# A one-core gated cross-attention and mixture-of-experts layer: reciprocals taken at step 19 of a turn instead of 13, and the sync queue's transfers in another order

## The reference, cut to what matters

```python
x = x + tanh(g_xattn) * xattn(layernorm(x), ctx)     # 32 batches of 128 x 512
x = x + tanh(g_ffn) * ffn(layernorm(x))

def xattn(x1, x2):                 # 8 heads of 16 channels, 512 positions, 128 channels
    q, k, v = proj(x1), proj(x2), proj(x2)
    attn = softmax(q @ k.T / 4)    # per head, 512 x 512
    return attn @ v

def ffn(x):                        # rmsnorm, router, top 2 of 8 experts, and a shared expert
    h = rmsnorm(x)
    return sum_of_top2(w_e * expert_e(h)) + shared(h)
```

## Time and profile before

| what | us |
|---|---|
| median of 3 runs | 1573.99 |
| lowest and highest of the 3 | 1565.47, 1575.32 |
| the profiled execution, its own time | 1563.96 |
| its span in the profile | 1562.1 |
| mean granted TensorE clock, as a share of the full one | 0.955 |

### The profile page before, as it was taken

The page is one execution under the profiler, slowest core; times in us unless marked ns, Lnnn a source line. Parts: engine busy times, 40 slices in busy tenths (PEclk is TensorE's granted clock), DMA queues, the critical chain, the costliest instruction groups (busy, mean ns, idle before and its releaser), DMA issues.

```text
span 1562.1 us, 25157 instructions
## 1 busy us (share of the span) xinstructions
PE 1411.3 (90%) x7290; PEld 669.2 (43%) x7290; DVE 1001.2 (64%) x2173; ACT 881.2 (56%) x1720; POOL 868.8 (56%) x1278
## 2 busy tenths in 40 slices
PE   4888899898998888888899989889999999999997
PEld 1122222222222222222222222226778888888886
DVE  5877677877787777777788777784675433333332
ACT  2467666775676666666677667673433433333333
POOL 7336655666566666566757664544321455555553
PEclk9999989998999999999999999999999999999999
DMA  5547555565766657567566666526655488976665
GB/s 168 155 137 197 160 170 161 170 178 154 155 168 172 168 157 157 150 174 183 163 164 180 169 153 149 143 98 196 143 138 174 93 215 206 221 177 129 110 112 83
DMA packets 161314, 247.94 MB, mean 159 GB/s; under 512 B 33606, under 2 KB 58829, under 8 KB 161183
## 3 DMA queue, kind: packets, MB, share of 16 engines
q1 hardware_dynamic: 138830, 208.43, 49.3%
q0 software_dynamic: 18256, 37.38, 12.8%
q10 hardware_dynamic: 4096, 0.53, 0.3%
HBM read 141.85 MB, written 103.88 MB: 157 GB/s over the span
## 4 chain that ended last, share of the span: by engine, by line
PE 43%; DMA 21%; issue 12%; POOL 7%; SPq 7%; DVE 5%; ACT 3%; POOLq 1%; ACTq 1%; DVEq 0%
PE bank L1409 15%; PE bank L1366 9%; DMA pv_d<-arena 7%; PE bank L1337 6%; SPq L466 6%; PE bank L1315 6%; DMA parts_k<-arena 4%; DMA arena<-m_rows 4%; DVE row_max L883 3%; DMA arena<-pv_d 3%; PE bank L1353 2%; POOL xs L768 2%; POOL arena L667 2%; POOL arena L664 2%; PE bank L1297 2%
## 5 line engine op out<-in xcount | busy, mean ns | idle before, releaser
L883 DVE TENSOR_REDUCE row_max<-bank 128x1 f32<-128x512 f32 x1024 | 670.9, 684 | 142.0 <-PE bank L1315 125.2
L1154 ACT ACTIVATE arena<-bank 128x512 f32<-128x512 f32 x1024 | 576.7, 603 | 321.6 <-PE bank L1337 310.6
L1337 PE MATMUL bank<-arena 112*128 112x512 bf16 x1024 | 331.5, 405 | 14.8 <-DMA arena<-m_rows 9.0
L1315 PE MATMUL bank<-arena 48*128 48x512 bf16 x1024 | 213.0, 412 | 105.0 <-DVE row_max L883 101.5
L1366 PE MATMUL bank<-arena 128*32 128x512 f32 x2048 | 297.3, 655 | 1.0 <-ACT arena L1154 0.7
L664 POOL TENSOR_TENSOR arena<-arena 128x512 bf16<-128x512 f32 x62 | 71.8, 1157 | 257.3 <-ACT arena L1146 254.8
L780 POOL DMA_INDIRECT out<-xs,ids x71 | 112.5, 1585 | 173.0 <-ACT xs L1238 138.1
L1337 PEld LDWEIGHTS bank<-arena 112*128 112x128 bf16 x1024 | 86.4, 103 | 252.5 <-ACT arena L1154 182.4
L1315 PEld LDWEIGHTS bank<-arena 48*128 48x128 bf16 x1024 | 49.6, 93 | 336.6 <-DVE row_max L883 258.0
L1409 PE MATMUL bank<-w_ring,h_hi 128*128 x568 | 183.0, 403 | 0.0
L1227 ACT ACTIVATE arena<-bank 128x256 f32<-128x256 f32 x103 | 39.5, 384 | 189.5 <-PE bank L1409 189.5
(11 more groups left out here) (176 smaller groups left out, 1981.3 us busy)
## 6 DMA issues: line engine op xcount, KB each, us to landing
pv_d<-arena SPq DMA_DIRECT2D x32, 512.0 KB, 4.7
w_ring<-split_d SPq DMA_DIRECT2D x60, 256.0 KB, 4.1
parts_k<-arena SPq DMA_DIRECT2D x96, 128.0 KB
arena<-parts_k SPq DMA_DIRECT2D x64, 192.0 KB
parts_q<-arena SPq DMA_DIRECT2D x96, 128.0 KB
arena<-parts_q SPq DMA_DIRECT2D x64, 192.0 KB
arena<-in_w SPq DMA_DIRECT2D x36, 256.0 KB, 4.6
arena<-in_ctx SPq DMA_DIRECT2D x32, 256.0 KB, 3.1
```

Of the source, the lines that this page charges most:

```text
L883: nc.vector.reduce_max(row_max[b % 2][:, at:at + 1], m_ps[(STEPS * b + u) % M_BANKS][:], AX_X).then_inc(s_mx, 1)
L1154: nc.scalar.activation(probs[group % 3][:, j, :], e_ps[n % E_BANKS][:], ACT.Exp, scale=float(DH) ** -0.5).then_inc(s_exp, 1)
L1315: nc.tensor.matmul(m_ps[(n + a) % M_BANKS][:], q_stack[b % 3][rows, h, qt * P:(qt + 1) * P], k_stack[b % 3][rows, h, :], start=True, stop= ...
L1337: nc.tensor.matmul(e_ps[n % E_BANKS][:], k_stack[b % 3][0:SHIFTED, h, kt * P:(kt + 1) * P], q_stack[b % 3][0:SHIFTED, h, :], start=True, s ...
```

## The change

`RECIP_AT` goes from 13 to 19, so VectorE's `invert` stands behind the maximum of step 19. There the loop first issues the reciprocal and then begins the rows of maxima for the same step. In each turn SP's order becomes: the queries' high part written, the values' product stored, the keys read, the queries' middle and low parts written, the denominators read, the queries read, context loaded, turned tokens stored, and only then the reciprocals stored and the values loaded. The amount of work and of data is the same.

```diff
-RECIP_AT = 13
+RECIP_AT = 19
...
             for i in TURNS:
                 if is_b(i + 2):
-                    read(i + 2, 0)
+                    write(i + 2, 1, HI)
                 if is_b(i - 1):
                     store_values(i - 1)
                 if is_b(i + 2):
-                    write(i + 2, 1, HI)
+                    read(i + 2, 0)
+                    write(i + 2, 1, MID)
+                    write(i + 2, 1, LO)
                 if is_b(i - 1):
                     load_denominators(i - 1)
                 if is_b(i + 2):
-                    write(i + 2, 1, MID)
-                if is_b(i - 1):
-                    store_reciprocals(i - 1)
-                if is_b(i + 2):
-                    write(i + 2, 1, LO)
+                    read(i + 2, 1)
                 if is_b(i + 4) and i + 4 >= 2:
                     load_ctx(i + 4)
                 if is_b(i - 3):
                     store_turned(i - 3)
-                if is_b(i + 2):
-                    read(i + 2, 1)
                 if is_b(i - 1):
+                    store_reciprocals(i - 1)
                     load_values(i - 1)
```

## The result

The changed kernel takes 1473.61 us (median of 4 runs, 1469.73 to 1477.03), against 1571.24 us for the kernel before on the same chip (4 runs, 1565.47 to 1575.32). The ratio is 0.938, with a 95% interval from 0.9337 to 0.9423: 6.2% faster. The forecast was 1465, inside a range of 1436 to 1515. The profiled execution took 1475.64 us, with a span of 1473.8, so its 88 us against the profiled execution of before can be followed in the trace.

The account below looks back on a forecast made before the run. PE, busy 90%, was held back by VectorE's reciprocal waiting for the denominators' DMA and by the low clock behind the pauses. 1563.96 - 104.7 (29 turns) + 3.1 (start) = 1462.4 us, put at 1465; range 1436 to 1515.

Parts of the forecast that it names:

- The reciprocal's wait: VectorE's wait for the denominators' DMA, 73.7 us in 25 waits, goes entirely at step 19, 3.9 us behind the landing.
- SP's order alone: With the new queue order but the reciprocal still at step 13, half a microsecond of its wait would be left.
- The pauses and the clock: PE's pauses behind the reciprocal's wait lower its clock; the mean over turns 1 to 29 rises from 0.93 to 0.98 or more.
- the sum from the other side: Cross-check of the gain: 73.7 us of reciprocal waits plus 65 us lost at the low clock, together 139 us.
- The turn: Turns 1 to 29 fall from 31.9 to 28.3 us each: 27.5 without pause plus 0.8 for new waits; 104.7 us less.
- turn 21: Check of 27.5: taken as a turn whose reciprocal did not wait; it took 29.40 us, 1.9 put down to pause and clock.
- the reciprocals' store: SP stores the reciprocals at 653.4 in turn 18, landing 1.4 us later; the values' load issues at 654.9 instead of 656.83.
- The start: Six key reads stand ahead of the queries' middle and low parts, delaying the first scores by 3.1 us; bounds 0 to 4.4.
- Turn 30 and the rest: Turns 30 and 31 and the experts' part keep their length, without key reads left or not using the changed lines.
- Rivals 1 and 2: Rows of maxima land late: at a turn's end (1485 to 1541 us, chance 0.17) or in mid-turn (1634 us, 0.05).
- rival 2: The first pair of rows of maxima lands behind the values' store, stopping PE for exponentials: 1634 us, chance 0.05.
- Rival 3: No change: the wait moves to step 19, or another loop as long as 31.9 us stands behind; 1563 to 1577, chance 0.04.

## Why the prediction was right, and where it was off

- **The reciprocal's wait.** The forecast had it near 0 at step 19. It went from 73.7 to 0.9 us. The working behind it was too optimistic: the denominators' read was forecast at T+9.4 and its landing at T+11.4. It was issued at T+10.9 in turn 17, and by the semaphore's events in the trace it landed 2.9 to 4.5 us behind its issue in turns 1 to 29, where it was 2.0 to 2.1 before. The margin at step 19 is 1.7 us in the median, and nothing at its least, instead of 3.9. The wait went because six steps left room for an error of some 2 us. The sentence that SP's order alone would leave half a microsecond fell: it left about 3.2 us in each turn, and 0.994 of the time.
- **The pauses and the clock.** Mean PEclk was forecast at 0.98 or more and came to 1.00. The low clock gave back 59.1 us of PE's busy time, where the sum from the other side had 65. The Trainium skill's "HAM oscillation" in "TensorE: Matmul & The Clock Gate" charges half of the throttled time; these traces agree with the charge within 10%. With all of the waits on top that working made 1428 us, and 1475.64 was measured, because waits came back in another place.
- **The turn.** Forecast 28.3 us, measured 28.57: 29 x 0.27 = 8 us short, the largest miss in the turns. The 0.8 us a turn that the forecast kept for new waits should have been 1.2 us over the 27.38 us at which the best turns of several kernels stand (it took 27.5 for that). That 27.5 was a good guess with a weak check: turn 21 is not one of the four whose reciprocal did not wait, for it waited 0.21 us. The four are turns 12, 16, 23 and 27, and they lasted 29.5 to 29.8 us. The step that failed is the reciprocals' store. It was forecast at T+16.3, landing after 1.4 us, and the load at T+17.8, sooner than before. It was in fact issued at T+18.5 and landed 4.2 us later, and the load went out at T+22.7, later than the T+19.7 of before (medians of turns 1 to 29: T+21.3 before, T+23.3 after). Two things were mis-sized. The query reads ended at T+17.4 (559.20) and not at T+15.4, since the key reads began 0.8 us later than forecast and took 4.92 us instead of 4.36, and the low part's write then took 2.8 us from its end to the first read (552.63 to 555.43) instead of 2.2. And 1.4 us was the landing of that small store with one write of a query part ahead of it in the queue, issued 1.7 us earlier; behind six reads SP's next issue, which waits for it, came 3.2 to 5.9 us later in turns 1 to 29. The forecast even claimed that POOL would get its load sooner. The run with the store in the middle bears on this term by changing it: beside the changed kernel on one chip it is worth 47 us. Of the 5.0 us by which the values' load was late against the forecast, 2.3 are the store's later issue and the rest its longer landing.
- **The start.** Forecast +3.1, measured +2.4 to turn 1. The first scores began at 32.47 us instead of 29.60, 2.9 us later, for the reason given: the six key reads stand between the query parts (the chain of waits and the timeline of PE). The forecast's 3.1 rests on a misread row: 19.09 is the start of the low part's issue, and the working set the end of the new one, 22.1, against it. Start against start it makes 21.5 - 19.09 = 2.4 us, and the new issue began at 21.65. That 3.1 came close to the 2.9 is luck.
- **Turn 30 and the rest.** The forecast kept them unchanged. Turn 30 grew by 4.8 us, and that was missed: the last load of values lands late there too, VectorE's moments wait 3.6 us for POOL, and PE, idle behind them, then runs at the low clock. The rows are VectorE's and PE's, in that order.

```profile
925.85 0.69 DVE L844 BATCH_NORM_STATS2 stats<-xs 128x6 f32<-128x512 f32 x1 [3.58 <-POOL xs L673]
```

```profile
927.32 0.61 PE L1312 MATMUL bank<-arena 48*128 48x512 bf16 x2 [4.19 <-DVE row_max L880]
927.86 1.94 PE L1363 MATMUL bank<-arena 128*32 128x512 f32 x8
```

- **Rivals 1 and 2** came to nothing. The rows of maxima waited for nothing in these turns, and their landing became steadier, not later (min, median, max, against 1.8/4.4/10.1 in the earlier trace rows):

```profile
DMA to landing us min/median/max: 2.3/4.4/6.3
```

For rival 2 the forecast named a rule of the Trainium skill ("DMA: Bandwidth & Descriptors", "Queues, rings and completion order"): a semaphore's increment lands only behind all earlier writes of the same DMA engine. No row shows the rows' landing tied to the store of the values ahead of them; their longest landing fell. What the rule says of a single DMA engine was not tried here. The 1.3 us of low clock in that rival's price is worked out from no row.
- **Rival 3**, the wait that moves to step 19, did not come. Its second half did, in small: another loop was right behind, at 28.6 and not at 31.9 us.

What stays open: why the load of the values lands anywhere from 6.1 to 9.6 us behind its issue in turns 1 to 29 of the changed kernel (6.1 to 12.2 us before, and 12.6 and 12.4 us in two turns of the first run with the store in the middle). No run took that apart. Nor is it shown why the small transfers land later under the new order, and no run moved the router's operations away from the rows of maxima alone, to win back the loss at step 22.

## What to carry to other kernels

A wait that is taken off an engine has to be followed through the queue of the engine that issues its transfers: the step alone and the order alone gained 2.1 and 0.6%, both together 6.2%. When it is gone, walk the next loop in the same way, store, landing, load, consumer, with landing times measured under the same traffic. And a wait that appears at a new instruction (the moments here) may be only where a loop surfaces: moving that instruction gained nothing, and issuing the loop's store 3 us sooner, with the reciprocal a step earlier, gained 3%.

## What the runs showed of the hardware

**Small VectorE operations beside a large one on POOL.** Of the changed kernel, turn 12, first POOL's and then VectorE's timeline:

```profile
415.50 1.28 POOL L702 TENSOR_TENSOR arena<-arena 128x512 f32<-128x512 f32 x1
416.86 1.27 POOL L709 TENSOR_TENSOR staged_lo<-arena,staged_hi 128x512 fp32r<-128x512 f32 x1
```

```profile
416.28 0.16 DVE L955 RECIPROCAL meta<-route 128x4 f32<-128x4 f32 x1
...
417.08 1.07 DVE L956 TENSOR_TENSOR meta<-route,meta 128x4 f32<-128x4 f32 x1
```

The reciprocal with one input of four numbers took 0.16 us while POOL worked. The tensor-tensor of the same size took 1.07 us and ended at 418.15, 0.02 us behind POOL's L709 (418.13). Its counterpart before took:

```profile
459.56 0.15 DVE L959 TENSOR_TENSOR meta<-route,meta 128x4 f32<-128x4 f32 x1
```

Over the router's tensor-tensor operations in the changed kernel's trace: 24 that began while POOL ran a tensor-tensor took 0.82 us on average (1.19 at most), 14 beside POOL's tensor-scalar 0.38, and 66 beside neither 0.19 us. 12 reductions and 5 reciprocals beside POOL kept their 0.17 and 0.16 us. But one input alone does not protect an operation. This cast began beside POOL's L709 in turn 17, and ended 0.02 us behind it; beside nothing it took 0.16 us:

```profile
560.98 1.02 DVE L963 CAST slots<-route 128x4 int32<-128x4 f32 x1
```

The Trainium skill names this contention for VectorE instructions with two SBUF inputs or in a 2-port perf mode ("GPSIMD Engine Reference", "1. Specifications"). The trace agrees for the two inputs; in which mode the cast ran it doesn't show. The later router steps showed the effect again by turning long operations short and short ones long.

**A 16 KB store behind six strided reads.** On SP's queue the reciprocals' store landed 1.4 us behind its issue before (3.0 at most), with one write of a query part ahead of it. In turns 1 to 29 of the changed kernel, where the six query reads stand ahead, SP's next issue, which waits for the landing, came 3.2 to 5.9 us behind it. The last three stores of the same trace, with no query reads left, landed in 1.7 to 3.0 us. The 16 KB read of the denominators went the same way: 2.0 to 2.1 us before, 2.9 to 4.5 us in turns 1 to 29 of the changed kernel, directly behind two writes of query parts, and 2.0 us again in the last three turns (semaphore events of the two traces). In turn 17 of the changed kernel SP stood idle for the store from 560.97 to 564.54. With the store in the middle of those reads the load's issue follows 3.65 us behind the store's (547.95 to 551.60), with other issues in between nearly to its end. What moved above all was the store's issue, and that brought the gain. Whether it is the reads ahead or other traffic that holds the store was not tried by itself.
